# Routed gate and up projections of layer 0 with the weights as the stationary operand

## What is computed

```python
scores = jax.nn.sigmoid(logits)
topk_w, topk_i = jax.lax.top_k(scores, TOPK)            # TOPK = 2, E = 8
gate = jax.nn.silu(jnp.einsum('th,eih->tei', xt, wg))   # i = 640, h = 256
up = jnp.einsum('th,eih->tei', xt, wu)
expert_out = jnp.einsum('tei,ehi->teh', gate * up, wd)
out = jnp.einsum('te,teh->th', comb, expert_out)        # plus the shared experts
```

## Time and profile before

| | us |
|---|---|
| median of 3 runs | 927.01 |
| lowest, highest | 918.31, 930.27 |
| the profiled execution, its own time | 925.53 |
| span of its trace | 923.7 |
| PE busy, of the span | 775.8 (84%) |
| DVE busy | 546.7 (59%) |
| ACT busy | 336.2 (36%) |
| mean granted TensorE clock | 0.925 of full speed |

### The profile page before, as it was taken

One profiled execution on the slowest core, in us unless ns is written; L12 is line 12 of the kernel. 1 busy time (PEld: TensorE's weight loads), 2 busy tenths in 40 slices (PEclk: granted clock), 3 DMA queues, 4 the chain that ended last, 5 costly groups with the idle time before them and its releaser, 6 DMA issues. The chain is left out here.

```text
span 923.7 us, 13581 instructions
## 1 busy us (share of the span) xinstructions
PE 775.8 (84%) x4383; PEld 483.8 (52%) x4383; DVE 546.7 (59%) x1333; ACT 336.2 (36%) x774; POOL 255.3 (28%) x316
## 2 busy tenths in 40 slices
PE   4888957999998999997778998899797169999980
PEld 1444536887565666663345555455454136555650
DVE  3789846533332222224889999999964525444545
ACT  1455434332232222212256656666653012222220
POOL 2343420520000000006543344544524202322332
PEclk8999967999999999999899999999986569999995
DMA  9355441390289999818400011110311069999926
GB/s 336 146 223 205 163 157 52 111 367 1 89 299 345 382 318 315 292 57 217 143 1 17 7 36 38 35 41 23 122 74 52 26 221 320 307 323 316 329 90 238
DMA packets 57097, 157.90 MB, mean 171 GB/s; under 512 B 7180, under 2 KB 36748, under 8 KB 51708
## 3 DMA queue, kind: packets, MB, share of 16 engines
q1 hardware_dynamic: 51700, 141.96, 44.1%
q0 software_dynamic: 5328, 15.08, 4.5%
HBM read 114.20 MB, written 42.81 MB: 170 GB/s over the span
## 5 line engine op out<-in xcount | busy, mean ns | idle before, releaser
L1245 PE MATMUL ps<-f_rg,f_xT 128*128 128x512 f32 (+1 forms) x276 | 111.8, 528 | 4.4 <-DMA f_rg<-w_routed 3.8
L1148 DVE TENSOR_TENSOR f_rh<-f_gate,ps 128x256 f32<-128x256 f32 (+1 forms) x69 | 26.0, 377 | 122.7 <-ACT f_gate L977 80.6
L2059 ACT ACTIVATE b_PX<-ps 128x512 f32<-128x512 f32 x128 | 72.8, 597 | 45.1 <-PE ps L2294 43.2
L1784 DVE TENSOR_REDUCE b_smax<-ps 128x4 f32<-128x1024 f32 x64 | 77.7, 1214 | 14.8 <-PE ps L2270 14.8
L2556 POOL DMA_INDIRECT y<-f_ys,f_to x47 | 45.1, 959 | 113.3 <-DVE f_ys L2605 109.9
L1245 PEld LDWEIGHTS ps<-f_rg,f_xT 128*128 128x128 f32 x276 | 52.5, 192 | 32.9 <-issue 23.9
L977 ACT ACTIVATE f_gate<-ps 128x256 f32<-128x256 f32 (+1 forms) x69 | 24.1, 349 | 123.7 <-PE ps L1245 123.2
L2294 PE MATMUL ps<-b_Q,b_Cx 100*128 100x256 f32 x256 | 56.2, 325 | 9.3 <-ACT b_PX L2059 6.7
L1547 POOL MEMSET b_half<- 128x1 f32 x1 | 0.1, 98 | 224.3 <-POOLq L66 224.3
L1268 PE MATMUL ps<-f_rd,f_rhT 128*128 128x256 f32 x230 | 60.9, 380 | 0.3 <-issue 0.3
L2574 ACT ACTIVATE f_gate<-ps 128x224 f32<-128x224 f32 x47 | 16.8, 357 | 113.2 <-PE ps L2652 113.2
(11 more groups left out here) (321 smaller groups left out, 1737.4 us busy)
## 6 DMA issues: line engine op xcount, KB each, us to landing
f_rg<-w_routed SPq DMA_DIRECT2D x23, 1280.0 KB, 7.8
rows<-a_blank SPq DMA_DIRECT2D x16, 1152.0 KB
rw<-w_ffn SPq DMA_DIRECT2D x24, 704.0 KB
f_rw<-w_ffn SPq DMA_DIRECT2D x23, 704.0 KB
f_rd<-w_routed SPq DMA_DIRECT2D x23, 640.0 KB, 5.4
f_xs<-rows SPq DMA_DIRECT2D x47, 144.0 KB
f_yk<-y SPq DMA_DIRECT2D x8, 512.0 KB, 7.1
raw<-w_shared SPq DMA_DIRECT2D x10, 384.0 KB
```

Source lines behind the costliest of these rows:

```text
L1245: mm = nc.tensor.matmul(ps[:, u % 4, 0:2 * n], xT[b % 2][:, c, :], rg[b % R_SLOTS][:, off:off + 2 * n], start=(c == 0), stop=(c == C - 1))
L1784: nc.vector.tensor_reduce(smax[t % 2][:, k // C, k % C, :], ps[:, FIRST:FIRST + 2, :].rearrange("p u (g n) -> p (u g) n", g=2), AX, ALU.ma ...
L2059: nc.scalar.activation(PX[g % RING][:].rearrange("p c m -> p (c m)"), ps[:, RETS + G_TURN[g] % 2, :], ACT.Exp, scale=XSC).then_inc(turn_re ...
```

## The change

The gate and up product swaps its operands. Each 128 columns of the weights become stationary, and `xT[c]` (128 rows) moves; the bank then holds inner feature by row, in n/128 chunks for gate and as many for up. Silu and product work on the same shapes as before, and the product is written straight into `rhT`. `turn_h`, `keep_hT`, the buffers `rh`, and the semaphores `h_turned` and `h_kept` go. `routed_down` waits for the product (`r_h`) and follows at a distance of two units, where it was three (`D_LAG`), which moves `keep_y` a unit ahead in DVE's order too. The product waits for `r_down` of unit u - 3, as there are three `rhT` buffers. The layout of the weights in DRAM and all DMAs stay as they are.

```diff
-    T_LAG, D_LAG = 2, 3
+    D_LAG = 2
...
-        rh = [sb(f"rh{n}", [P, 256]) for n in range(2)]
...
-            def keep_hT(u):
-                n = PARTS[u % PER][1]
-                act.wait_ge(h_turned, u + 1)
-                if u >= 3:
-                    act.wait_ge(r_down, u - 2)
-                nc.scalar.copy(rhT[u % 3][:].rearrange("p c t -> p (c t)")[:, 0:n], ps[:, 4 + u % 2, 0:n]).then_inc(h_kept, 1)
...
                 dve.wait_ge(r_silu, u + 1)
-                if u >= 2:
-                    dve.wait_ge(h_turned, u - 1)
-                nc.vector.tensor_tensor(rh[u % 2][:, 0:n], gate[u % 2][:, 0:n], ps[:, u % 4, n:2 * n], ALU.mult).then_inc(r_h, 1)
+                if u >= 3:
+                    dve.wait_ge(r_down, u - 2)
+                nc.vector.tensor_tensor(rhT[u % 3][:].rearrange("p c t -> p (c t)")[:, 0:n], gate[u % 2][:, 0:n],
+                                        ps[:, u % 4, n:2 * n], ALU.mult).then_inc(r_h, 1)
...
-                for c in range(C):
-                    off = c * 2 * I0 + 2 * at
-                    mm = nc.tensor.matmul(ps[:, u % 4, 0:2 * n], xT[b % 2][:, c, :], rg[b % R_SLOTS][:, off:off + 2 * n],
-                                          start=(c == 0), stop=(c == C - 1))
+                for k in range(2 * n // P):
+                    for c in range(C):
+                        off = c * 2 * I0 + 2 * at + k * P
+                        mm = nc.tensor.matmul(ps[:, u % 4, k * P:(k + 1) * P], rg[b % R_SLOTS][:, off:off + P], xT[b % 2][:, c, :],
+                                              start=(c == 0), stop=(c == C - 1))
                 mm.then_inc(r_scored, 1)
-
-            def turn_h(u):
...
             def routed_down(u):
                 b, i = u // PER, u % PER
                 at, n = PARTS[i]
-                pe.wait_ge(h_kept, u + 1)
+                pe.wait_ge(r_h, u + 1)
...
-                if u >= T_LAG:
-                    turn_h(u - T_LAG)
                 if u >= D_LAG:
                     routed_down(u - D_LAG)
-            for u in range(RU - T_LAG, RU):
-                turn_h(u)
-                routed_down(u - 1)
-            routed_down(RU - 1)
+            for u in range(RU - D_LAG, RU):
+                routed_down(u)
```

More of the change, by code:

```diff
@@ L838, in routed_experts @@
         r_h = sem("r_h")
-        h_turned = sem("h_turned")
-        h_kept = sem("h_kept")
         r_down = sem("r_down")
@@ L977, in _ @@
                 nc.scalar.activation(gate[u % 2][:, 0:n], ps[:, u % 4, 0:n], ACT.Silu).then_inc(r_silu, 1)
-                if u >= T_LAG:
-                    keep_hT(u - T_LAG)
-            for u in range(RU - T_LAG, RU):
-                keep_hT(u)
         @block.vector
@@ L1242, in routed_gate_up @@
                     pe.wait_ge(r_h, u - 3)
-                for c in range(C):
-                    off = c * 2 * I0 + 2 * at
-                    mm = nc.tensor.matmul(ps[:, u % 4, 0:2 * n], xT[b % 2][:, c, :], rg[b % R_SLOTS][:, off:off + 2 * n],
-                                          start=(c == 0), stop=(c == C - 1))
-                mm.then_inc(r_scored, 1)
-            def turn_h(u):
[L1250 to L1256, removed]
+                for k in range(2 * n // P):
[3 more added lines that the diff above has]
+                                              start=(c == 0), stop=(c == C - 1))
+                mm.then_inc(r_scored, 1)
             def routed_down(u):
```

## The result

The changed kernel takes 920.38 us (median of 20 runs, 916.39 to 924.46) against 926.46 us for the kernel before (median of 20), a ratio of 0.9938 with a 95% interval of 0.9916 to 0.9959. That is 6.1 us less; 5.0 were forecast, and 921.5 as the time. It lies within 2%, as forecast, and inside the range.

What follows compares the result with a forecast made beforehand. The prediction took PE's issue in the routed blocks as the bound. Work -10.3, new wait +6.4, stage end -0.4 and DMA waits -0.7 gave -5.0 us; it said 921.5 us, range 912 to 935.

Steps and rivals of the forecast that it cites:

- The bound: Routed blocks: PE's issue bounds them, a block lasting the sum of start-to-start distances, 7.24 us counted against 7.23.
- The swapped product: Gate and up: 40 load-and-matmul pairs a block at 0.11 us, 4.40 us, 0.10 more than now; five transposes, 0.55, go.
- the ratio of 2.5 a column: Gate and up: estimate from the skill's page for short pairs, 4.3 us becoming some 10; no row showed it.
- The wait that takes its place: First down of each block but the first waits for `keep_y`'s copy: 0.29 us, 22 times, +6.4 us.
- The end of the stage: Behind the last unit: PE's 0.35 us wait for a copy of `rhT` goes, two downs hide the product, -0.4 us.
- DMA: PE's 3.8 us of waits for weights: earlier `r_down` sends stores and loads sooner, -0.7 us, bounds -3.8 to +2.
- The start of the stage: First routed block, in the half clock granted just before 240 us: costs the same by columns.
- The sum: Whole kernel: -10.3 + 6.4 - 0.4 - 0.7 = -5.0 us, forecast time 921.5 us.
- A: Rival, down product: the wait for `y_kept` does not come, block 6.8 us, kernel 913 us; chance 0.20.
- B: Rival, gate and up: short pairs run above 0.11 us, no gain at 0.117, about 935 us at 0.13; chance 0.15.
- C: Rival, gate and up: weight loads not hidden at all, 7.6 us more a block, +170 us, 1090; chance 0.02.
- D: Rival, routed blocks: transfers bind, DMA share full at 6.4 us a block; only caps A, no chance of its own given.

Runs made afterwards that it cites:

- two banks: Changed kernel with a block's sums alternating between PSUM banks 7 and 4, so down waits for the copy of the block before the last; ratio 0.9863.
- spread stores: Changed kernel with the image's four 400 KB stores issued behind blocks 2, 10, 13 and 16 instead of all behind block 2; ratio 0.9892.
- distance of three: Changed kernel with the down product three units behind again, four buffers for its operand and one PSUM bank for the sums; ratio 0.9945.
- 64 columns: Changed kernel with 64 instead of 128 moving columns in gate and up, half of each block's rows left out; a single run, 913.67 us.
- distance of three, stores spread: Changed kernel with down three units behind, four buffers, one bank, and the image's stores behind blocks 2, 10, 13 and 16; ratio 0.9866.
- long matmuls: Changed kernel with gate and up operands as before the change (rows stationary, weights moving) and no turning at all; ratio 0.9879.
- transposes back: Changed kernel with five transposes a block put back on PE in front of the down products, results unused; ratio 0.9988.
- distance of three, the second: Changed kernel with down three units behind, image stores behind blocks 2, 13, 16 and 19, second context copy behind block 9 instead of 6; ratio 0.9856.
- changed kernel again: The changed kernel run once more unaltered, on another chip, against the kernel before; ratio 0.9903.

## Why the prediction was right, and where its terms were off

*The bound.* PE's issue sets the block: held. The transposes that were put back cost what PE's distances say, with ACT's copies still gone.

*The swapped product.* A pair costs 0.111 us, not 0.110, and the gate and up product of a block 2 x 1.78 + 0.89 = 4.45, not 4.40: the work that goes is 0.40 a block instead of 0.45, 9.2 us instead of 10.3. The reading from four pairs of another stage was enough. The rule of the Trainium skill (TensorE: Matmul & The Clock Gate, "The mechanism", the section ahead of the one that the prediction names) that loads overlap only in other row groups does not hold in this trace: 920 loads start 0.111 apart beside matmuls on the same 128 rows. Nor does the ratio of 2.5 a column, worked out from the figures of its section "Back-to-back issue gap": 4.45 against 4.30.

*The wait that takes its place.* It came where it was put and is shown by the run with two banks: 7.06 - 6.84 = 0.22 us a block, not 0.29, so 22 x 0.22 = 4.8 us instead of 6.4. The term that was off is the time from the end of the copy to the load, 0.12 in the row of layer 1 and 0.06 here (343.38 to 343.44). These two sizes err by 1.1 and 1.6 us in opposite directions, so that work, wait and end together, -4.3 us in the forecast, came out at -4.8. That part of the closeness is luck.

*The end of the stage.* Ten down matmuls now stand in one group behind the last unit, without the 0.35 us of the earlier trace rows; this term was not tested alone.

*DMA.* I counted on -0.7. PE's idle time for weights was 3.8 us and is 2.1 and 2.2 in the two traces of the changed kernel, so about -1.7. But a wait also costs what the clock does behind it. By the distances between the transposes the waits cost 4.3 us before, and 4.0 in the first trace of the changed kernel, where the clock fell, and 2.4 in the second, where it did not: so -0.3 or -1.9, with -0.7 between them. That the image's burst makes the wait is shown by the spread stores. That the earlier release shortens it is shown in part: the image goes out 26.2 us into the stage, where it was 29.3, 1.5 of them from the half clock; but in the run with the distance of three most of the first wait's growth was PE's earlier demand. In the prediction the shorter distance looked mostly like a cost, and by that run it was even.

*The start of the stage.* The prediction left the half clock at the start as it was. It was absent in both traces of the changed kernel and came again with the same code in the run with the stores spread, so no run shows that the change removes it; it is 1.5 us of the difference between the two traces.

*The sum.* -9.2 + 4.8 - 0.4 - 1.7 = -6.5 us, against 6.1 between the medians. The traces bear out the first three: without the waits for weights and without the clock the stage is 4.6 us shorter. The -1.7 has no such standing, so that the sum comes this near to the medians is partly luck. The stage's 6.5 us in the traces are made up otherwise: 4.6, 0.3 and 1.5 of clock at its start.

*The rivals.* A (no wait) fell, and two banks show what it would have been: 0.986, 12 to 13 us, near its 913. Its own reasons, that the copy starts earlier or PE looks ahead, did not come. B (pairs slower than 0.117) fell, and was a fair worry: the 64 columns show that the load has no spare. C and D fell (C's price was low in its own terms, 7.6 x 23 is 175 us); with two banks the DMA engines still carried a block of 6.84 us.

## What to carry to other kernels

When a helper step goes and the step behind it is moved up, look at what else hangs on that distance: here the copy of the sums came onto the path, and the waits for weights became shorter; the one cost 4.8 us, the other gave much of it back, and only changing each alone told them apart. A second PSUM bank in place of the freed one was worth about as much as the change itself (0.22 us a block). Stores in small pieces between the loads took away a wait that cost 2.4 us, or 4.0 with the clock behind it; that is a reading of traces, as their effect on the whole time was not clear of the difference between chips. To turn an operand by swapping a float32 product cost 0.13 us in a block of 7 with 128 moving columns; with 64, the pace of the loads was paid, 0.108 us a pair.

## What the hardware showed that I had not expected

*A short wait can cost twice.* In the changed kernel the wait ahead of block 6 is followed by a stretch at half the granted clock (1.2 instead of 2.4 GHz). The timeline of PE and the stretch:

```profile
279.09 3.29 PE L1233 MATMUL ps<-f_xT,f_rg 128*128 128x128 f32 x16 [2.07 <-DMA f_rg<-w_routed]
```

```profile
279.70:283.10 3.40, 3.40 (x17) 3.31 (x17) 0.27 (x1) 0.38 (x1) 0.00 (x0) 0.50 0.97 401
```

Sixteen pairs take 3.29 us where 1.95 is usual, and the way to the next unit's first pair is 1.7 us too long. The same kernel on another chip waited 2.17 us and kept the full clock (2.05 us for the pairs), and the kernel before waited 2.94 and kept it too. All traces together have ten waits for weights of over 1.6 us. The clock fell behind those of 2.04 (64 columns), 2.07 (changed kernel), 2.07 (distance of three, stores spread), 2.38 (long matmuls) and 3.67 us (distance of three), and stayed behind those of 1.69 (transposes back), 2.08 (distance of three, the second), 2.17 (changed kernel again), 2.49 (two banks) and 2.94 us (before). Whether it falls is therefore not told by the length of the wait alone; what else decides is open. It means that part of what the expectations call waits for weights was clock: of the 4.0 us of the changed kernel 2.2 were wait and 1.7 clock, and the 7.8 of the distance of three, the 4.0 of the same with spread stores, and the stage of the long matmuls hold a fall as well.

*A long stretch at half clock.* With 64 moving columns the stage began with 13.7 us at half clock, PE shown as busy all the time:

```profile
234.60:248.30 13.70, 13.70 (x60) 12.98 (x59) 2.22 (x6) 2.47 (x5) 0.00 (x0) 0.50 0.28 97
```

None of the other traces has more than 3.4 us of it there. This is one trace, so that the 64 columns are the cause is not shown. It is most of the reason why that run's stage is 172.1 us with a shorter block.
